# Gated mixtures: the low part of a tile's up-weights copied by ScalarE, the high part by VectorE

## The reference, cut to what matters

```python
# _L0_ffn_ref: E = 8 experts, top 2, D = F = 128
scores = softmax(xt @ gate_w.T)
idx = top_k(scores + gate_b, 2)
cw = sum(one_hot(idx, E) * weights, axis=1)
h1 = einsum('td,efd->etf', xt, w1) + b1
h3 = einsum('td,efd->etf', xt, w3) + b3
a = swiglu(h1 * h3)          # min(g, 7) * sigmoid(1.702 g) * (clip(l, -7, 7) + 1)
y = einsum('etf,edf->etd', a, w2) + b2
out = einsum('te,etd->td', cw, y) + shared expert
...
x = x + 0.5 * _L0_ffn_ref(_layernorm(x), ...)
x = x + _L0_attn_ref(...)
x = x + 0.5 * _L0_ffn_ref(_layernorm(x), ...)
```

## Time and profile before

| | |
|---|---|
| runs, median (lowest to highest) | 2554.82 us (2554.65 to 2556.2) |
| profiled execution, span | 2555.3 us |
| busy: PE, PEld | 2005.7 us (78%), 1619.8 us (63%) |
| busy: DVE | 1955.3 us (77%) |
| busy: ACT | 1416.9 us (55%) |
| busy: POOL | 1039.6 us (41%) |
| tile loop of g0 | from 149 to 268 us |
| tile loop of g1 | from 1141 to 1262 us |

### The profile page before, as it was taken

One profiled execution on the slowest core, in us unless ns is written; L12 is line 12 of the kernel. 1 busy time (PEld: TensorE's weight loads), 2 busy tenths in 40 slices (PEclk: granted clock), 3 DMA queues, 4 the chain that ended last, 5 costly groups with the idle time before them and its releaser, 6 DMA issues. The chain is left out here.

```text
span 2555.3 us, 85621 instructions
## 1 busy us (share of the span) xinstructions
PE 2005.7 (78%) x34294; PEld 1619.8 (63%) x34294; DVE 1955.3 (77%) x4641; ACT 1416.9 (55%) x2304; POOL 1039.6 (41%) x961
## 2 busy tenths in 40 slices
PE   3779399999999998669578994764666667769994
PEld 3668388888888887558457993552222234547894
DVE  5889589999999997779764444597999978855443
ACT  1647244444444443447455551367999978737452
POOL 3757355544444453666565662004000000036563
PEclk7889699999999998679879996685555578869997
DMA  5133200000000000022332222003333200031324
GB/s 124 47 98 111 86 3 0 0 0 0 0 0 0 0 0 3 31 82 88 117 105 81 70 69 81 0 0 52 63 50 63 35 2 1 2 90 46 92 77 122
DMA packets 103658, 120.90 MB, mean 47 GB/s; under 512 B 23224, under 2 KB 85288, under 8 KB 102848
## 3 DMA queue, kind: packets, MB, share of 16 engines
q1 hardware_dynamic: 82544, 80.39, 13.1%
q0 software_dynamic: 18176, 37.79, 4.4%
q10 hardware_dynamic: 2768, 0.55, 0.2%
HBM read 60.00 MB, written 46.20 MB: 42 GB/s over the span
## 5 line engine op out<-in xcount | busy, mean ns | idle before, releaser
L2521 DVE CUSTOM_DVE_ANT_0 be_logs<-be_joint,be_logs 128x1024 f32<-128x1024 f32 x256 | 293.3, 1222 | 10.2 <-ACT be_logs L2504 9.2
L2504 ACT ACTIVATE be_logs<-be_joint,b_tiny 128x1024 f32<-128x1024 f32 x256 | 283.7, 1114 | 19.7 <-PE be_joint L2489 11.8
L2489 PE MATMUL be_joint<-be_parts_k,be_parts_q 64*128 64x512 f32 x512 | 202.3, 789 | 108.9 <-DVE be_sums L2521 91.4
L446 POOL DMA_INDIRECT d_pairs<-s_y_tile,s_x_tiles x156 | 178.7, 1145 | 128.9 <-DVE s_y_tile L1404 104.4
L2489 PEld LDWEIGHTS be_joint<-be_parts_k,be_parts_q 64*128 64x128 f32 x512 | 73.7, 285 | 237.3 <-DVE be_sums L2521 216.5
L1764 POOL TENSOR_TENSOR m_roped_q<-m_raw_q,kg_xn 128x512 f32<-128x512 f32 x64 | 82.4, 1288 | 327.0 <-ACT m_raw_q L1686 327.0
L559 POOL IOTA s_xn<- 128x32 int32 x2 | 0.5, 253 | 487.1 <-POOLq L63 487.1
L446 POOL DMA_INDIRECT d_pairs<-g_y_tile,g_x_tiles x156 | 158.0, 1013 | 92.4 <-ACT g_y_tile L894 60.9
L1404 DVE TENSOR_SCALAR s_y_tile<-s_ps_y,s_x_tiles 128x128 f32<-128x128 f32 x156 | 47.5, 346 | 149.1 <-PE s_ps_y L1238 149.1
L1238 PE MATMUL s_ps_y<-s_down,s_a_tile 128*128 x1248 | 151.7, 275 | 0.0
L1238 PEld LDWEIGHTS s_ps_y<-s_down,s_a_tile 128*128 128x128 f32 x1248 | 145.9, 192 | 0.0
(11 more groups left out here) (501 smaller groups left out, 6303.7 us busy)
## 6 DMA issues: line engine op xcount, KB each, us to landing
g_x_tiles<-d_rows SPq DMA_DIRECT2D x78, 132.0 KB, 2.1
s_x_tiles<-d_rows SPq DMA_DIRECT2D x78, 132.0 KB, 2.1
d_rows<-d_rows SPq DMA_DIRECT2D x32, 132.0 KB
s_down<-L_ffn_We SPq DMA_DIRECT2D x16, 256.0 KB, 6.0
be_parts_q<-be_high_q SPq DMA_DIRECT2D x64, 64.0 KB, 2.3
be_parts_q<-b_soft_q SPq DMA_DIRECT2D x64, 64.0 KB, 2.3
be_parts_k<-be_high_k SPq DMA_DIRECT2D x60, 64.0 KB, 2.3
be_parts_k<-b_soft_k SPq DMA_DIRECT2D x60, 64.0 KB, 2.3
```

The lines of the kernel that those rows point to most:

```text
L446: nc.gpsimd.indirect_dma_start(out=pairs[:, :], out_offset=bass.IndirectOffsetOnAxis(ap=x_tile[i % LOADS_AHEAD][:, h, D:D + 1].bitcast(U32 ...
L2489: last = nc.tensor.matmul(joint_ps[k % DEPTH][:, a, :], parts[b % 2][0][rows, i * P:(i + 1) * P], parts[b % 2][1][rows, half * 512:(half + ...
L2504: nc.scalar.activation(logs[k % DEPTH][:, :, :], joint_ps[k % DEPTH][:, :, :], ACT.Ln, bias=A.tiny[:, :]).then_inc(s.log_ready, 1)
L2521: nc.vector.tensor_tensor_reduce(out=flat, in0=joint_ps[k % DEPTH][:, :, :].rearrange("p a j -> p (a j)"), in1=flat, scale=1.0, scalar=0.0 ...
```

## The change

ACT gets a `tile_weights` of its own: it copies the low part (index 1 of the second dimension) of the expert's up-weights for tile i+1, between `tile_out(i-3)` and the wait for the product of tile i. For that it loads the 39 expert numbers into registers before the loop, after waits for the table and for the last low part of the weights, and copies tiles 0 and 1 ahead of its first rounding. DVE's copy keeps the high part only, in the same place as before. PE waits for one semaphore more, `tile_w_low`, at the head of `tile_above`. What is computed, and every other instruction, stays.

```diff
--- before.py
+++ after.py
@@ -683,7 +683,7 @@
         y_tile = [sb(f"y_tile{i}", [P, HALVES, D]) for i in range(Y_TILES)]
         back = [shared[:, 0:E, :].rearrange("p k (t d) -> p (k t) d", d=D), r.xn[:, 1, :, 0:D]]
         s = stage_sems(nc, ctx, f"g{call}", DISPATCH_SEMS + " prods_ready sig_ready linear_ready gate_ready a_ready third_ready small_in "
-                       "tile_third tile_prod_g tile_prod_l tile_sig tile_linear tile_gate tile_a", h_full=4, tile_h=2, rows_in=LOADS_AHEAD, y_sent=Y_TILES, back_in=4)
+                       "tile_third tile_prod_g tile_prod_l tile_sig tile_linear tile_gate tile_a tile_w_low", h_full=4, tile_h=2, rows_in=LOADS_AHEAD, y_sent=Y_TILES, back_in=4)
         dispatch = GatedDispatch(nc, X, r, s, c, d, w, K.rows)
         block = ctx.enter_context(nc.Block())
 
@@ -763,6 +763,7 @@
             def tile_above(i):
                 b = i % 2
                 pe.wait_ge(s.tile_w, i + 1)
+                pe.wait_ge(s.tile_w_low, i + 1)
                 pe.wait_ge(s.tile_low, i + 1)
                 if i < 2:
                     pe.wait_ge(s.third_ready, 2 * TRIPS)
@@ -895,6 +896,17 @@
                                          scale=x_tile[i % LOADS_AHEAD][:, h, D + 1:D + 2]).then_inc(s.tile_y, 1)
 
             act.wait_ge(s.bias_ready, 1)
+            act.wait_ge(s.table_ready, 1)
+            act.wait_ge(s.w_low, NE)
+            experts = tile_values(nc, mybir.EngineType.Activation, r.tile_expert, MAX_TILES, E)
+
+            def tile_weights(i):
+                wait(act, s.tile_h[1], i - 1)
+                nc.scalar.copy(up_tile[i % 2][:, 1, :, :, :].rearrange("p a b f -> p (a b f)").unsqueeze(1),
+                               up[:, :, 1, :, :, :].rearrange("p e a b f -> p e (a b f)")[:, bass.ds(experts[i], 1), :]).then_inc(s.tile_w_low, 1)
+
+            tile_weights(0)
+            tile_weights(1)
             tile_high(0)
             for i in range(MAX_TILES):
                 b = i % 2
@@ -907,6 +919,8 @@
                                          bias=tile_bias[:, part, i:i + 1]).then_inc(s.tile_third, 1)
                 if i > 2:
                     tile_out(i - 3)
+                if 0 < i and i + 1 < MAX_TILES:
+                    tile_weights(i + 1)
                 act.wait_ge(s.tile_prod_g, i + 1)
                 wait(act, s.tile_gate, i - 1)
                 nc.scalar.activation(sig_tile[b][:, :], prod_tile[b][:, 0, :], ACT.Silu, scale=SHARP).then_inc(s.tile_sig, 1)
@@ -1009,8 +1023,8 @@
 
             def tile_weights(i):
                 wait(dve, s.tile_h[1], i - 1)
-                nc.vector.tensor_copy(up_tile[i % 2][:, :, :, :, :].rearrange("p m a b f -> p (m a b f)").unsqueeze(1),
-                                      up[:, :, :, :, :, :].rearrange("p e m a b f -> p e (m a b f)")[:, bass.ds(experts[i], 1), :]).then_inc(s.tile_w, 1)
+                nc.vector.tensor_copy(up_tile[i % 2][:, 0, :, :, :].rearrange("p a b f -> p (a b f)").unsqueeze(1),
+                                      up[:, :, 0, :, :, :].rearrange("p e a b f -> p e (a b f)")[:, bass.ds(experts[i], 1), :]).then_inc(s.tile_w, 1)
 
             def tile_low(i):
                 dve.wait_ge(s.tile_high, i + 1)

```

## The result

The changed kernel takes 2566.41 us in the median of 7 runs (2561.64 to 2570.65), the kernel before, run beside it, 2556.2 (2554.15 to 2560.16, 7 runs). The ratio is 1.0045 with a 95% interval of [1.0033, 1.0057]: slower by 8.4 to 14.6 us. The forecast was slower by 6.4, with 2567 as the upper end of its range. The profiled execution has a span of 2567.8 us, before 2555.3.

A forecast was written before the change was run, and what follows sets the result against it. VectorE was taken to set the pace before, a loop through TensorE and ScalarE's copy after: 2.92 us a tile gives +4.66 and +2.67, the ends -0.95, together +6.4 on 2554.82, so 2561.2 us; range 2557.5 to 2567.

The forecast's parts named there:

- the loop: Gated stages' tile loops: TensorE's start, third factors, output rows, ScalarE's copy, TensorE's next start; 2.92 us a tile.
- the sum: Both gated stages: 35 tiles at 2.92 us give +4.66 and +2.67, the ends -0.95; together +6.4 us.
- the first tiles: Start of each gated stage: shorter loop without output rows, old pace about holds; unchanged within 0.2 us.
- The copy, from a row of the same shape: Loop term: ScalarE's copy of 512 elements a partition, taken from a 128x512 copy elsewhere in the kernel; 0.60 us.
- The overlap with the operation before it: Loop term: ScalarE's copy starts before the output-row operation ahead of it has ended; minus 0.10 us.
- ScalarE's end to TensorE's load: Loop term: from the end of ScalarE's copy to TensorE's first weight load of the next tile; 0.05 us.
- TensorE to third factors and third factors to the end of the output rows: Two loop terms: TensorE's first load to third factors 1.02 us, from there to the output rows' end 1.35 us.
- the end: Last tiles of both gated stages: GpSimd is no longer behind in writing out tiles, giving back 0.95 us.
- A: Tile loops: ScalarE's idle time covers the copy; 2.52 us a tile, 20 us less, 2535 us; chance 0.07.
- B: Tile loops: same mechanism, longer through address arithmetic or semaphore; another 0.09 us a tile, 2567.5 us; chance 0.10.
- C: Tile loops: loop a little shorter than summed, under 2.90 us a tile; 2558.5 to 2559.9 us; chance 0.20.
- D: Tile loops: TensorE's clock falls during its waits; up to 71 us, some 40 if half the time, 2600; chance 0.03.

The follow-up runs named there:

- e1: Changed kernel with ScalarE's copy moved ahead of the two output-row operations; 0.999 of the kernel before, most frequent period 2.43 to 2.44 us a tile.
- e3: Changed kernel with ScalarE copying 256 elements in place of 512, VectorE the other 768; 1.0029 of the kernel before, most frequent period 2.73 to 2.74 us.
- e4: Changed kernel with VectorE copying all 1024 elements and ScalarE's copy going to a tile nobody reads or waits for; 1.001 of the kernel before.
- i0_changed: The changed kernel unaltered, run again beside the follow-up kernels; 1.001 of the kernel before, in a trace of 2665.4 us with stops.

## Why the prediction was right in its direction and short in its size

**Right: the loop.** That the copy fits in ScalarE's idle time, that VectorE is relieved, and that the period nevertheless grows because the copy stands behind the third factors and the output rows and TensorE waits for it: each link is in the rows after, and the periods of e1 (0.5 off for the output rows), e3 (0.21 off for 256 elements) and e4 (nothing where nobody waits) show it by removal; their times don't. As forecast are also VectorE's 0.417 us for half the copy, the even starts of tiles, ScalarE in one piece from L918 to L926, and the 1.12 us between output rows and GpSimd in the last tiles. TensorE's wait before a tile was forecast at 0.3 to 0.5 us and is 0.71. The kernel before waits in two places, 0.19 us ahead of L776 and 0.33 ahead of the down-projection L792 (means over the first loop); the second wait is gone, and its time and the 0.16 of the longer period come on top of the first, 0.68 in all.

**The step that failed** is the sum: it came to +6.4 us, and the two stages grew by 9.9. Terms of the loop were mis-sized, above all the copy, put at 0.60 us and measured at 0.632; and the first tiles, put at nothing, measured +1.3 us.

**Short: the terms of the loop.** Forecast 2.92, measured 103.22 / 35 = 2.949.
- The copy, from a row of the same shape: forecast 0.60, measured 0.632. Its value in the earlier trace rows is of a copy behind another operation, L859, and from a fixed address; the two of the 18 with nothing just ahead of them took 0.618. In the tile stages the same copy takes 0.61 to 0.62 at the start of the stage (613 ns at least) and behind the third factors (e1, median 617), and 0.63 behind the output rows. +0.03.
- The overlap with the operation before it: forecast 0.10, measured 0.12 to 0.13 (212.81 + 0.62 against 213.31). -0.03.
- ScalarE's end to TensorE's load: forecast 0.05, measured 0.07. +0.02.
- TensorE to third factors and third factors to the end of the output rows: 1.03 and 1.35, where the forecast had 1.02 and 1.35. +0.01.

Together +0.029 a tile, and over 70 tiles +2.0 us.
The estimate of 0.613 us from the Trainium skill, "VectorE: DVE Perf Modes", in its section on the TRN2 errata, fits the shortest copy, 613 ns; behind the output rows the trace shows 632, and the measurement decides.

**Wrong: the first tiles.** The prediction took them as unchanged, because the loop without output rows is 0.5 us shorter and "the old pace about holds". But the old pace there wasn't 2.79. From the first low part of the input to the third factors of tile 3 the kernel before took 9.55 and 9.56 us, the changed one 10.12 and 10.30: +1.3 us. The distances between the first tiles were 2.44, 2.23, 2.70 and 2.65, 2.01, 2.72, and are now 2.99, 2.42, 2.43 and 2.99, 2.44, 2.58. The 2.43 is the loop of e1, without output rows. The 2.99 of the very first is TensorE's clock. Windows of the first stage, from the first weight load on, before and then after:

```profile
149.02:151.70 2.68, 2.65 (x12) 2.68 (x13) 0.42 (x1) 1.18 (x3) 0.00 (x0) 0.50 0.80 227
151.70:154.30 2.60, 2.12 (x18) 1.89 (x16) 2.19 (x6) 1.42 (x4) 0.00 (x0) 0.97 0.55 159
```

```profile
149.47:154.30 4.83, 4.80 (x22) 4.83 (x23) 2.16 (x6) 1.90 (x6) 0.00 (x0) 0.50 0.73 203
```

The stage begins at a granted clock of 0.50, the 1.2 GHz level. In the kernel before it is at 1.00 from 151.84 on, as tile 1 begins, in the changed one only from 154.35 on, when the third factors of tile 1 have begun: from the first load of tile 1 to its third factors it is 1.25 us before and 1.74 after. In the second stages it rose 3.77 us (before, first distance 2.65) and 6.14 us (after, 2.99) behind the first load. The change doesn't fix this moment: the same changed kernel had first distances of 2.64 and 2.46 in i0_changed, where the clock rose after 3.75 and 3.33 us. So of the 1.3 us some 0.9 (2.99 - 2.44 and 2.99 - 2.65) are a late rise of the clock, and 0.4 are left for the change.

**Nearly right: the end.** From tile 38 to the end, the stages give back 0.55 and 0.23 us, 0.78 in place of 0.95: +0.2.

The bridge: 6.4 + 2.0 + 1.3 + 0.2 = 9.9 us, the measured 9.92 of the two stages.

**The rivals.** A, the offload works, is refuted for this place of the copy: 2.95 in place of 2.52. Its remark that a copy under 0.49 us would bring the period below the mean of before is borne out by e3 in the periods, 2.74 at 0.42 us; a gain in time wasn't seen. The rule of the Trainium skill, "Perfetto Trace Analysis", section Optimizing Scalar/DVE Operations, that with VectorE saturated work may go to ScalarE, isn't enough here: VectorE was busy for 95% of the first loop, and the time rose by 0.45%. B, a longer loop from the address or the semaphore, has the size (2567.5) but not the cause: the semaphore gave 0.02 of the 0.09, and the address no more than the 0.01 by which the shortest copy (0.613) exceeds the forecast's 0.60; e3's 2.74 is the 2.32 of the loop without a copy and the 0.42 of its own. C, a shorter loop, didn't come. D, the clock, didn't come in the steady part of the changed kernel's loops (1.00 in both windows), but the low level lasted longer at the start of both stages, for some 0.9 us, and it came back behind the stops of the experiments.

The range, 2557.5 to 2567, held the changed kernel's median of 2566.41, but 1.0045 of the 2556.2 measured beside it is 2567.7, 0.7 above its end (of the 2554.82 that the forecast started from it is 2566.3). The upper end was made of the loop's term alone, with 2.96 a tile; the first tiles, for which I allowed 0.2 us, should have widened it by one or two us upwards.

## What to carry to other kernels

An engine's idle time is no room for an operation as such: ask who waits for its result, and what stands ahead of it on the engine. If the next unit's start on another engine waits for it, the period can't be shorter than that loop, and every operation ahead of the copy that the next unit's start doesn't wait for, here the output rows at 0.50 us a tile, belongs behind it. Here that move is shown in the periods (2.44 in place of 2.95) and not yet in the time of the kernel. When a loop is summed from durations of rows, take them from rows in the same company (behind the same kind of operation), and sum the first units of the stage apart, with the clock that they have.

## What the runs showed of the hardware that was not expected

- The same program took 2554 to 2560 us beside the first run of the changed kernel and 2643 to 2680 beside the others. The traces of these others have stops of 1 to 3 us about every second or third tile in the tile stages, in the second stage at the same tiles in traces of five chips; i0_changed lost no time where the program runs in loops. With them a difference of 0.2 us a tile, and even of 0.5, all but vanished from the time.
- After a stop of 2.5 us TensorE's granted clock was 0.52 for 3.5 us, and weight loads took 0.33 us in place of 0.19.
- At the start of the tile stages the granted clock was 0.50 and rose 2.82 to 6.14 us behind the first load (before and changed kernel, first runs); the distance of the first two tiles went with it, 2.44 to 2.99 us.
- A copy of 128x512 on ScalarE took 0.602 us in the first phase behind L859, 0.613 at least in the tile stage, 0.617 in the median behind the third factors (e1) and 0.632 behind two operations on output rows, and began 0.12 to 0.13 us before the end of these.
